# Basis steps ahead of three transformer layers: the row is picked by TensorE's stationary operand, done columns are zeroed in the rows, and the power gives the norm itself

## The reference

```python
mod = silu(c) @ w_mod + b_mod        # one such product for each of the three layers
...                                  # three layers of attention and MLP
U, _ = jnp.linalg.qr(P)              # P is (288, 64), the same for all 32 samples
A = zeros.at[iu, ju].set(v).at[ju, iu].set(-v)   # v = silu(c) @ W.T + b, 64 x 64 for each sample
R = expm(A)
z = einsum('btn,nd->btd', x, U)
x = x + einsum('btd,nd->btn', z @ R - z, U)
```

## Time and profile before

| | us |
|---|---|
| median of 3 runs | 5081.57 |
| the profiled execution | 5082.07 |
| its span, first to last instruction | 5080.30 |
| first basis step, copy of `vs` begins | 9.95 |
| last basis step, update of `G` begins | 427.76 |

### The profile page before, as it was taken

The page is one execution under the profiler, slowest core; times in us unless marked ns, Lnnn a source line. Parts: engine busy times, 40 slices in busy tenths (PEclk is TensorE's granted clock), DMA queues, the critical chain, the costliest instruction groups (busy, mean ns, idle before and its releaser), DMA issues. The chain is left out here.

```text
span 5080.3 us, 125326 instructions
## 1 busy us (share of the span) xinstructions
PE 4506.7 (89%) x46073; PEld 3767.7 (74%) x46073; DVE 3663.6 (72%) x7723; ACT 2273.7 (45%) x3828; POOL 1139.6 (22%) x2044
## 2 busy tenths in 40 slices
PE   6654899999999986999999999958999999999998
PEld 4543688888888875888888888757777777777776
DVE  5665788888888864676676676657777777777774
ACT  0111555555555534555554554424444444444443
POOL 1001222222222222222222222212222222222221
PEclk7576899999999997999999999978999999999999
DMA  3001100101010011101101000010000000000000
GB/s 71 20 1 41 35 25 28 28 28 28 28 28 28 26 35 44 29 28 28 28 28 28 28 28 27 22 51 23 23 25 22 25 22 25 22 25 22 25 20 18
DMA packets 122230, 141.59 MB, mean 28 GB/s; under 512 B 14446, under 2 KB 117780, under 8 KB 122112
## 3 DMA queue, kind: packets, MB, share of 16 engines
q1 hardware_dynamic: 121968, 139.75, 10.0%
q10 hardware_dynamic: 144, 0.22, 0.0%
HBM read 110.87 MB, written 29.06 MB: 28 GB/s over the span
## 5 line engine op out<-in xcount | busy, mean ns | idle before, releaser
L867 DVE TENSOR_REDUCE mx<-S 128x4 f32<-128x1024 f32 x768 | 920.5, 1217 | 80.3 <-PE S L1105 77.4
L629 ACT ACTIVATE pT<-S 128x1024 f32<-128x1024 f32 x768 | 745.3, 1022 | 366.5 <-PE S L1131 362.3
L577 ACT ACTIVATE hf<-M 128x512 f32<-128x512 f32 (+1 forms) x480 | 266.7, 556 | 1159.8 <-PE M L1185 672.4
L504 POOL TENSOR_SCALAR hh<-hf 128x512 fp32r<-128x512 f32 (+1 forms) x480 | 280.4, 584 | 1170.0 <-ACT hf L577 1127.2
L1131 PE MATMUL S<-qT,kT 32*128 32x256 f32 x9216 | 427.9, 296 | 64.8 <-ACT pT L629 63.4
L1105 PE MATMUL S<-kT,qT 32*128 32x256 f32 x3072 | 370.9, 336 | 84.3 <-DVE mx L867 45.9
L1131 PEld LDWEIGHTS S<-qT,kT 32*128 32x128 f32 x9216 | 331.2, 185 | 137.0 <-ACT pT L629 91.8
L1144 PE MATMUL A<-pT,V 128*32 128x256 f32 x6144 | 414.7, 388 | 19.5 <-ACT pT L629 19.5
L858 DVE TENSOR_TENSOR hl<-hf,hh 128x512 fp32r<-128x512 f32 (+1 forms) x480 | 323.8, 676 | 114.0 <-POOL hh L504 112.0
L1185 PE MATMUL M<-xh,w_hi 128*128 128x256 f32 x1728 | 393.7, 310 | 3.3 <-POOL xh L480 3.3
L1105 PEld LDWEIGHTS S<-kT,qT 32*128 32x128 f32 x3072 | 224.1, 189 | 206.2 <-DVE mx L867 82.1
(11 more groups left out here) (229 smaller groups left out, 10151.8 us busy)
## 6 DMA issues: line engine op xcount, KB each, us to landing
mid<-xbo SPq DMA_DIRECT2D x64, 288.0 KB, 3.2
xld<-mid SPq DMA_DIRECT2D x64, 288.0 KB, 3.0
xa<-mid SPq DMA_DIRECT2D x64, 288.0 KB, 3.5
gA<-gates SPq DMA_DIRECT2D x96, 144.0 KB, 3.3
gM<-gates SPq DMA_DIRECT2D x96, 144.0 KB, 3.0
xld<-in_x_dram SPq DMA_DIRECT2D x32, 288.0 KB, 3.5
xa<-in_x_dram SPq DMA_DIRECT2D x32, 288.0 KB, 3.5
out_dram<-xbo SPq DMA_DIRECT2D x32, 288.0 KB, 2.2
```

The source lines that it names most:

```text
L504: pool.tensor_scalar(hh[:, 2 * f:2 * f + m, :].rearrange("p m c -> p (m c)"), hf[:, f % 2, 0:m * T], 1.0, 0.0, ALU.mult, ALU.add).then_inc ...
L577: act.activation(hf[:, f % 2, 0:c], MBANK[f % 2][:, 0:c], ACT.Gelu if rot else ACT.Gelu_apprx_tanh).then_inc(s["m_hf"], 1)
L629: act.activation(pT[:, g % 2, 2 * h:2 * h + 2, :], S[:, 2 * h:2 * h + 2, :], ACT.Exp, scale=float(HD) ** -0.5).then_inc(s["a_ex"], 1)
L867: dve.tensor_reduce(mx[:, p, :, :], S[:, r:r + 2, :].rearrange("p a (t k) -> p a t k", t=NT), AX.X, ALU.max).then_inc(s["a_mx"], 1)
```

## The change

The stationary operand of the spread is now `sel`, which ScalarE writes as `blockones` times column j of `eye2`: ones in row j of either block, zeros elsewhere. The moving operand is `G` itself, so `mk` and `mask` go. `sel` for step j+1 is written right behind the squares of step j. The zeros in the done columns of the lower half are written into `G`, one column a step. GpSimd raises to +1/2 and so delivers the norm. The sign goes by -1/2 or +1/2 times `house`, which is now 2; `sv` and `sw` hold twice the signed column values, made ahead of the wait for the power. `q[2]` and the correction of `vs` go.

```diff
+        sel = sb("sel", [P, P])
...
-        GS = 12
+        GS = 11
...
@@ gpsimd
-            own(pool.memset(house_row[ROT:ROT + 1, :], 1.0))
-            own(pool.memset(mask[ROT:P, 0:ROT], 0.0))
-            own(pool.memset(house[ROT:P, :], 1.0))
+            own(pool.memset(house_row[ROT:ROT + 1, :], 2.0))
+            own(pool.memset(flat_rows[ROT:P, :], 0.0))
+            own(pool.memset(house[ROT:P, :], 2.0))
...
-                pool.tensor_tensor(rt[:, :], n2[:, :], mhalf[:, 0:1], ALU.pow).then_inc(g_rt, 1)
+                pool.tensor_tensor(rt[:, :], n2[:, :], half[:, :], ALU.pow).then_inc(g_rt, 1)
...
@@ scalar
+            def select(j):
+
+                act.activation(sel[:, :], blockones[:, :], ACT.Identity, scale=eye2[:, bass.ds(j, 1)]).then_inc(g_sel, 1)
+
+            act.wait_ge(const, CONSTS)
+            select(0)
             act.wait_ge(load, 16 * 9)
             act.activation(sT[:, :, :], cT[:, :, :], ACT.Silu).then_inc(silu, 1)
 
             def length2(j):
 
-                act.wait_ge(g_step, j * GS + 2)
+                act.wait_ge(g_step, j * GS + 1)
                 act.activation(junk2[:, :], vs[:, :], ACT.Square, accum_out=n2[:, :]).then_inc(g_n2, 1)
+                select(j + 1)
...
@@ vector, basis_step
-                own(dve.scalar_tensor_tensor(out=mk[:, :], in0=G[:, :], scalar=col(eye2), in1=mask[:, bass.ds(ROT - j, D)],
-                                             op0=ALU.mult, op1=ALU.mult))
...
-                own(dve.tensor_scalar(q[1][:, :], col(vs), 0.0, 2.0, ALU.is_ge, ALU.mult))
-                own(dve.tensor_scalar(col(sg), q[1][:, :], -1.0, house[:, :], ALU.add, ALU.mult))
+                own(dve.tensor_scalar(col(sg), col(vs), 0.0, -0.5, ALU.is_ge, ALU.add))
+                own(dve.scalar_tensor_tensor(out=sv[:, :], in0=col(vs), scalar=house[:, :], in1=col(sg), op0=ALU.mult, op1=ALU.mult))
+                own(dve.scalar_tensor_tensor(out=sw[:, :], in0=col(G), scalar=house[:, :], in1=col(sg), op0=ALU.mult, op1=ALU.mult))
                 dve.wait_ge(g_rt, j + 1)
 
-                own(dve.scalar_tensor_tensor(out=q[2][:, :], in0=n2[:, :], scalar=rt[:, :], in1=col(sg), op0=ALU.mult, op1=ALU.mult))
-                own(dve.scalar_tensor_tensor(out=q[3][:, :], in0=col(vs), scalar=q[2][:, :], in1=n2[:, :], op0=ALU.mult, op1=ALU.add))
+                own(dve.scalar_tensor_tensor(out=q[3][:, :], in0=sv[:, :], scalar=rt[:, :], in1=n2[:, :], op0=ALU.mult, op1=ALU.add))
                 own(dve.reciprocal(q[4][:, :], q[3][:, :]))
-                own(dve.scalar_tensor_tensor(out=q[5][:, :], in0=col(G), scalar=q[2][:, :], in1=dot[:, :], op0=ALU.mult, op1=ALU.add))
+                own(dve.scalar_tensor_tensor(out=q[5][:, :], in0=sw[:, :], scalar=rt[:, :], in1=dot[:, :], op0=ALU.mult, op1=ALU.add))
                 own(dve.tensor_scalar(q[6][:, :], q[5][:, :], q[4][:, :], col(after), ALU.mult, ALU.mult))
 
-                own(dve.tensor_tensor(col(vs), col(vs), q[2][:, :], ALU.add))
                 own(dve.scalar_tensor_tensor(out=G[:, :], in0=vs[:, :], scalar=q[6][:, :], in1=G[:, :], op0=ALU.mult, op1=ALU.add))
+                own(dve.tensor_scalar(col(G), col(G), flat_rows[:, :], None, ALU.mult))
...
@@ tensor
-                pe.wait_ge(g_step, j * GS + 1)
-                pe.matmul(MBANK[1][:, 0:D], blockones[:, :], mk[:, :], start=True, stop=True).then_inc(g_vb, 1)
+                pe.wait_ge(g_sel, j + 1)
+                if not isinstance(j, int) or j:
+                    pe.wait_ge(g_step, j * GS)
+                pe.matmul(MBANK[1][:, 0:D], sel[:, :], G[:, :], start=True, stop=True).then_inc(g_vb, 1)
```

More of the change, by code:

```diff
@@ L1390, in preamble @@
         house_row = sb("house_row", [P, P])
-        eye2 = sb("eye2", [P, ROT])
+        eye2 = sb("eye2", [P, ROT + 1])
+        sel = sb("sel", [P, P])
         after = sb("after", [P, ROT])
-        mask = sb("mask", [P, ROT + D])
+        flat_rows = sb("flat_rows", [P, 1])
+        half = sb("half", [P, 1])
         house = sb("house", [P, 1])
         G = sb("G", [P, D])
-        mk = sb("mk", [P, D])
         vs = sb("vs", [P, D])
@@ L1403, in preamble @@
         sg = sb("sg", [P, ROT])
+        sv = sb("sv", [P, 1])
+        sw = sb("sw", [P, 1])
         q = [sb(f"q{i}", [P, 1]) for i in range(7)]
@@ L1419, in preamble @@
         e_out = sem("e_out")
-        g_mk = sem("g_mk")
+        g_sel = sem("g_sel")
         g_vb = sem("g_vb")
@@ L1427, in preamble @@
         u_rt = sem("u_rt")
-        CONSTS = 26
+        CONSTS = 27
         Q_FIRST, Q_MOD, Q_A, Q_TAYLOR, Q_SQUARE = 2, 6, 4, (2, 2, 2, 2, 2), 2
@@ L1482, in keep @@
                                        pattern=[[tilestep, view.shape[1]]], channel_multiplier=step))
-            for tile, value in ((ident, 0.0), (blockones, 0.0), (house_row, 0.0), (eye2, 0.0), (after, -1.0), (mask, 1.0),
-                                (mhalf, -0.5), (house, 0.0), (sign, 1.0)):
+            for tile, value in ((ident, 0.0), (blockones, 0.0), (house_row, 0.0), (eye2, 0.0), (after, -1.0), (flat_rows, 1.0),
+                                (mhalf, -0.5), (half, 0.5), (house, 0.0), (sign, 1.0)):
                 own(pool.memset(tile[:, :], value))
@@ L1653, in _ @@
             end = GS * ROT
-            dve.tensor_tensor(junk[0:ROT, 0:ROT], ABANK[1][0:ROT, 0:ROT], eye2[0:ROT, :], ALU.mult).then_inc(g_step, 1)
+            dve.tensor_tensor(junk[0:ROT, 0:ROT], ABANK[1][0:ROT, 0:ROT], eye2[0:ROT, 0:ROT], ALU.mult).then_inc(g_step, 1)
             dve.wait_ge(g_step, end + 1)
```

## The result

The changed kernel takes 5040.49 us, the median of 4 runs (5031.73 to 5042.60), against 5079.95 before (5077.63 to 5092.95, 4 runs). The ratio is 0.9914, 95% interval 0.9893 to 0.9934. A later repeat gives 5041.86 against 5080.94, ratio 0.9921 (0.9904 to 0.9938). The forecast was 5037. The profiled execution of the changed kernel, the fastest of its four, has a span of 5029.7 us, 50.6 less than before.

The account below looks back on a forecast made before the run. The preamble was taken as bound by one chain of steps, with no engine full and its gain passing to the end. Terms summing to 45.5 us, taken from the profiled 5082.1, gave 5037 us, range 5020 to 5056.

Parts of the forecast that it names:

- 29 plain steps: Plain preamble steps: `q[2]`, the `vs` correction and `mk` go, 0.77 us a step, 5.79 to 5.02; 22.3 us in all.
- into 20, 24, 28, 32: Steps after a chunk's end: the spread no longer waits behind the take-out; 2.16 us each, 8.6 us in all.
- second of a round (5): Second spread of a Taylor round: the chain arrives 0.77 us earlier, within TensorE's 0.86 idle; 3.8 us in all.
- second in the loop (9): Second steps in the loop: gains of 0.38 us from copy to `G` and 0.61 to the spread; 8.9 us in all.
- start, to the first copy of `vs`: Preamble start: first `sel` and a second table load delay the first spread from 8.54 to 9.86; loss 1.3 us.
- step 0's scalars, once more: Step 0: its own saved scalars, said to be in no other count, give 0.5 us back.
- spreads that lose the high level: Second spreads after 248.8 us: two of twelve at TensorE's high clock charged as falling to the low level; -1.2 us.
- The covers: Plain steps: `sv` and `sw` hide in the power wait by 0.06 us, `sel` ahead of the spread by 2 us.
- The early spread: Chunk ends: the spread runs under the take-out, `G` to copy falls from 4.18 to 2.48 us, gain 1.70 each.
- the rival of a dear +1/2: GpSimd's power in every step: +1/2 takes longer than 0.55 us; 5107 us at three times that; chance 4%.
- the rival too: Low-clock stretch, steps 14 to 36: busier TensorE gets its high clock, 13 us more gain, 5023 us; chance 12%.
- The layers as long as before: Layers behind the preamble: untouched by the change; a change of their 4647 us by more than a few would refute the forecast.

Follow-up runs that it names:

- where ScalarE zeroes: Changed kernel with the Silu ahead of the first `sel` and ScalarE, not VectorE, zeroing column j of `G` and `vs`; 5038.18 us, one run.
- The norm alone: Kernel before with only the arithmetic part: power +1/2, `sv` and `sw`, no `q[2]` or correction of `vs`; `mk` and `mask` stay; 5049.89 us, ratio 0.9939.
- `sel` alone: Changed kernel with the norm arithmetic of before (power -1/2, `q[2]`, correction of `vs`); 5068.28 us, ratio 0.9979 to the kernel before.
- The fillers: Changed kernel with one or two extra unused matmuls for each step of chunks 1 to 3; 5036.08 us with one, 5053.91 with two, one run each.
- factors first: Changed kernel with ScalarE zeroing columns, Silu before first `sel`, `Bk` and `Nk` before each Taylor round's squares; 5033.95 us (0.9903), repeat 5017.15 (0.9883).
- the two fillers: Changed kernel with two extra unused matmuls for each step of chunks 1 to 3; 5053.91 us, one run.

## Why the prediction was right

The times, 5040.49 and 5041.86 for a forecast of 5037, lie in the range, and the mechanism held: one chain of steps, shortened where the working said, with the gain passed on. That the sum of 45.5 us came so close to the preamble's 46.1 and 45.1 is in part luck, since errors in both directions cancelled. The working's terms, each over its intervals from copy of `vs` to copy of `vs`, against the two profiles of the changed kernel:

| term | predicted | changed | repeat |
|---|---|---|---|
| 29 plain steps | 22.3 | 20.8 | 19.9 |
| into 20, 24, 28, 32 | 8.6 | 8.7 | 8.7 |
| into 8 and 14 | 1.4 | 1.5 | 2.1 |
| first of a round (6) | 1.3 | 2.1 | 1.6 |
| second of a round (5) | 3.8 | 3.5 | 3.4 |
| second in the loop (9) | 8.9 | 9.1 | 9.0 |
| first in the loop, the last end | 1.2 | 1.7 | 1.7 |
| start, to the first copy of `vs` | -1.3 | -1.25 | -1.25 |
| step 0's scalars, once more | 0.5 | none | none |
| spreads that lose the high level | -1.2 | none | none |
| sum | 45.5 | 46.1 | 45.1 |

- *The preamble is one chain, and its gain passes to the end.* Held for the chain: 46.1 and 45.1 us, 45.5 predicted, and two parts that add up. How much of it reaches the end is known only within the layers' variation, below.
- *Step 0's scalars.* The working adds 0.5 us for them as "in no count above". But the interval into step 1 starts at the copy of step 0 and holds them, so they were counted twice: the intervals, the start and the end already make up the whole 46.1.
- *The plain step.* The mechanism was right in each part, the size of one off: I put the column at 0.26 to the spread, it took 0.36. I had taken the 0.05 between `mk` and its spread, and it is 0.15 now; up to the copy it is 0.07 more (1.56 for 1.49). That made the step 5.10 for 5.02 and cost 2 us. It is not the small instruction that does it: where ScalarE zeroes, `G` with its 128x288 stands right ahead of the spread and has the same 0.15 (63.06 to 63.21). The norm alone keeps the 0.05 and `sel` alone has the 0.15, so it comes with `sel`. The kernel before had it too, in step 2 for instance (`mk` ends at 20.07):

```profile
19.55 0.52 DVE L1566 SCALAR_TENSOR_TENSOR mk<-G,eye,mask 128x288 f32<-128x288 f32 x1
...
20.21 1.30 PE L1670 MATMUL M<-mk,blockones 128*128 128x288 f32 x2 [4.56 <-DVE mk L1566]
```

It is there in steps 0, 2, 8, 14, 20, 24, 28 and 32 and in no other step whose spread waits for `mk`. These are the steps where TensorE's program has one more wait (for `sT` or for weights) right ahead of the spread's own. With `sel` every spread has two waits, `g_sel` and `g_step`, and all plain steps have the 0.15. Two waits in a row are thus the suspect. No run took the second wait away, and in the squaring loop, where the spread has both too, the distance is 0.05; so it stays open.

- *The covers.* `sv`, `sw` and `sel` cost nothing outside the loop, but only just: `sw` ends 0.01 us ahead of the power, and from the copy of `vs` to `G` it is 2.78 us for 3.23, 0.45 less where 0.46 was foreseen. One place I had not priced: `sel` also stands ahead of `Bk` and `Nk` on ScalarE in the Taylor rounds. In the changed kernel VectorE still did not wait there; 0.6 us more on ScalarE made it wait.
- *The early spread.* Held to 0.02 us a step, and undoing it gave it back.
- *The start.* Predicted 9.86 (its parts add up to 9.83), measured 9.73. The Trainium skill's "ScalarE: Activation LUTs", What ACT_TABLE_LOAD costs, has about 1.28 us for the load and a drain of some 1.38 us with each switch of the set. The trace agrees with the load (8.10 to 9.38); no drain showed, `sT` starts at 9.40.
- *The power.* 551 ns, 553 before: the rival of a dear +1/2 falls.
- *The clock.* I charged 1.2 us for spreads that would lose the high level in the rounds. None was lost, and the sign was wrong: two of the 14 second spreads ran at the low level before (the steps into 53 and 61 took 6.16 and 6.20 us, the other second steps of the loop 5.62 to 5.75), and none ran wholly at it now. So about 1.1 of the 9.1 us in the loop are clock; the edit itself gives some 0.9 a step there, not 0.99. In the low stretch little changed: of the steps from 14 to 35 one, into 21, was shorter by the clock (4.83). The fillers speak against the rival too.
- *The layers.* "The layers as long as before" was true in the profile (4643 for 4648), but they vary by 11 us between the two profiles of the changed kernel and by 20 between those of factors first. The median gained 39.5 us where the preamble gained 46.1, in the repeat 39.1 for 45.1; with the norm alone it was 30.6 for 29.7, with factors first 47.0 for 60.2 and then 60.7 for 60.8. The differences are within the layers' variation, and no run here separates them from a real loss of a few us.

## What to carry to other kernels

Where no engine is full, write out one step from start to start: each instruction on the chain counts at its pitch, and what fits into a wait counts zero until the wait is used up. An edit that takes the last producer out from behind unrelated work can be worth more than the instructions it removes: a step at a chunk's end gained 2.2 us where a plain step gained 0.7, and 1.4 of that went with the early spread. When code that an edit does not touch varies by a good part of what the edit brings, compare a time stamp between the two parts beside the total. And a sum that comes out right is checked term by term, since a double count and a wrong sign can hide in it.

## What the runs showed of the hardware

- In the stretch of the two fillers the granted-clock column says 1.00 from 130 to 215 us, while each spread there takes 1.30 or 1.33 us, as at the low level. In that profile the column first falls below 1.00 between 220 and 225 us (0.56). Ahead of its first low entry the column was wrong here, and the durations told the level.
- From the end of VectorE's last instruction to the start of the spread lie either 0.05 or 0.15 us, and 1.49 or 1.56 to the copy, and the instruction's size (128x1 or 128x288) does not decide which. Outside the squaring loop the longer one stands wherever TensorE has a second wait right ahead of the spread's own.
- TensorE was at the low level for 85 us on end with 92% of its time busy, in matmuls of 96x32 and 128x128 and one spread of 128x288 a step.
- The power over 128x1 on GpSimd took 551 ns with the exponent +1/2 and 553 with -1/2.
- With an Identity ahead of the Silu, ScalarE loaded its tables twice (1.28 us each); with the Silu first, once for Silu, Identity and Square together.
